# Softmax denominators from sums of three, three and two key blocks, added in wide pieces, in a two-pass attention kernel on one core

## What is computed

```
q = Wq @ layernorm(x) + bq;  k = Wk @ ctx + bk;  v = Wv @ ctx + bv     # 512 x 1024 each
dot  = mask * (q . k) / sqrt(32) - (1 - mask) * 1e6                    # per head, 1024 x 1024
out  = (softmax(dot) * mask) . v
x    = x + tanh(g_xattn) * out
y    = fp8(layernorm(x) * scale) / scale
x    = x + tanh(g_ffn) * (y @ (fp8(W2 * scale1) / scale1))
```

## Time and profile before

| | |
|---|---|
| median of 3 runs | 2537.36 us (2537.34 to 2537.48) |
| span of the profiled execution | 2538.4 us |
| PE busy | 2479.6 us, 98% of the span |
| DVE busy | 1986.1 us, 78% |
| POOL busy | 1642.1 us, 65% |
| ACT busy | 1392.0 us, 55% |
| DMA engines, mean share in the attention slices | 4 to 5 tenths |

### The profile page before, as it was taken

How to read it: one execution, slowest core, us unless ns; L and a number is a source line. 1 busy time by engine, 2 the same in 40 slices (tenths; PEclk the granted TensorE clock), 3 DMA queues, 4 the chain that set the end, 5 groups by cost and what they waited for, 6 DMA issues and landing times.

```text
span 2538.4 us, 40565 instructions
## 1 busy us (share of the span) xinstructions
PE 2479.6 (98%) x13177; PEld 1380.4 (54%) x13177; DVE 1986.1 (78%) x3259; ACT 1392.0 (55%) x2606; POOL 1642.1 (65%) x1259
## 2 busy tenths in 40 slices
PE   7999999999999999999999999999999999999997
PEld 5888888874444444444444444444444444444442
DVE  6767667776788888888888888888888888888885
ACT  3333333315666665666666666666665666666664
POOL 2333333426777777777777777777777777777775
PEclk9999999999999999999999999999999999999999
DMA  6766666653444444444444444444444444444411
GB/s 239 256 244 239 237 237 237 215 183 88 94 97 97 100 102 94 96 91 94 91 97 93 91 91 91 91 91 90 99 91 92 95 99 100 97 98 99 101 47 55
DMA packets 241807, 313.48 MB, mean 123 GB/s; under 512 B 75000, under 2 KB 142648, under 8 KB 241624
## 3 DMA queue, kind: packets, MB, share of 16 engines
q1 hardware_dynamic: 230776, 275.56, 43.2%
q10 hardware_dynamic: 10848, 35.66, 3.9%
HBM read 199.83 MB, written 101.38 MB: 119 GB/s over the span
## 4 chain that ended last, share of the span: by engine, by line
PE 88%; DVE 6%; issue 3%; DMA 1%; POOL 1%; ACT 0%; SPq 0%; DVEq 0%; POOLq 0%; ACTq 0%
PE bank L863 20%; PE bank L848 20%; PE bank L893 19%; PE bank L878 17%; PE bank L904 8%; PE bank L941 4%; DVE part_max L1146 3%; PE bank L933 1%; POOL pair_sum L398 1%; DMA q_st<-qx_scr 0%; DVE y L101 0%; DMA w_nat<-in_L_xattn_Wk_dram 0%; DMA v_scr<-stage 0%; DVE isnan L100 0%; DVE x_raw L1046 0%
## 5 line engine op out<-in xcount | busy, mean ns | idle before, releaser
L398 POOL TENSOR_TENSOR pair_sum<-probs 128x512 f32<-128x512 f32 x1020 | 1279.6, 1287 | 430.8 <-ACT probs L715 430.8
L1146 DVE TENSOR_REDUCE part_max<-bank 128x1 f32<-128x512 f32 x2048 | 1283.0, 682 | 346.4 <-PE bank L878 338.1
L715 ACT ACTIVATE probs<-bank 128x512 f32<-128x512 f32 x2048 | 1071.3, 603 | 655.8 <-PE bank L863 647.4
L863 PE MATMUL bank<-q_st,k_st 100*128 100x512 f32 x2048 | 875.4, 429 | 5.2 <-ACT probs L715 5.2
L878 PE MATMUL bank<-k_st,q_st 98*128 98x512 f32 x2048 | 814.0, 397 | 8.7 <-DVE part_max L1146 6.2
L863 PEld LDWEIGHTS bank<-q_st,k_st 100*128 100x128 f32 x2048 | 386.5, 189 | 513.2 <-issue 270.8
L893 PE MATMUL bank<-probs,v_t 128*32 128x512 f32 x4096 | 546.3, 605 | 0.0
L878 PEld LDWEIGHTS bank<-k_st,q_st 98*128 98x128 f32 x2048 | 388.7, 190 | 112.6 <-DVE part_max L1146 8.7
L389 POOL TENSOR_TENSOR stage_lo<-stage,stage_hi 128x512 fp32r<-128x512 f32 x128 | 185.4, 1473 | 139.5 <-ACT stage_hi L661 138.6
L904 PE MATMUL bank<-pair_sum,ones 128*32 128x512 f32 x2040 | 266.4, 594 | 0.0
L661 ACT ACTIVATE stage_hi<-stage 128x512 fp32r<-128x512 f32 x128 | 80.2, 632 | 205.7 <-DVE stage L1010 143.1
(11 more groups left out here) (112 smaller groups left out, 1969.1 us busy)
## 6 DMA issues: line engine op xcount, KB each, us to landing
k_st<-k_scr SPq DMA_DIRECT2D x96, 512.0 KB
q_st<-q_scr SPq DMA_DIRECT2D x192, 256.0 KB
c_raw<-in_ctx_dram ACTq DMA_DIRECT2D x32, 512.0 KB, 7.1
k_scr<-stage_hi SPq DMA_DIRECT2D x64, 256.0 KB, 2.5
k_scr<-stage_lo SPq DMA_DIRECT2D x64, 256.0 KB, 2.8
v_scr<-stage SPq DMA_DIRECT2D x64, 256.0 KB, 2.9
q_scr<-stage_hi SPq DMA_DIRECT2D x64, 256.0 KB, 2.3
q_scr<-stage_lo SPq DMA_DIRECT2D x64, 256.0 KB, 2.5
```

The costliest lines, as they stand in the source:

```text
L398: nc.gpsimd.tensor_tensor(pair_sum[:, r % 2, h], probs[:, a, h], probs[:, a + 1, h], ALU.add).then_inc(pair_done, 1)
L715: nc.scalar.activation(probs[:, c % PR, h, :], s_bank_of(n, k)[:, :], ACT.Exp).then_inc(exp_done, 1)
L863: nc.tensor.matmul(s_bank_of(n, k)[:, :], k_st[p][0:KS, h, j * P:(j + 1) * P], q_st[p][0:KS, th, h, :], start=True, stop=True).then_inc(sc ...
L1146: nc.vector.tensor_reduce(part_max[:, th, sh, at:at + 1], x_bank_of(n, "tile", k)[:, :], AX, ALU.max).then_inc(max_done, 2)
```

## The change

- `add_pair` becomes `add_block`. The eight key blocks of a half are summed as (0, 1, 2), (3, 4, 5), (6, 7). The second block of a group is added to the first, out of `probs`, the third to the running `group_sum`. Each block is added in two pieces of two heads, 128 x 1024. That is 5 blocks, 10 pieces in a half, 20 in a quad.
- Denominator bursts: three for a half, at slots 19, 35, 43, 59 and, in the next quad, 3 and 11: 6 in a quad instead of 8. ACT's wait for a free place in `probs` goes by the new count of adds (`ADDED`).
- In `slot`, PV and denominator bursts now come ahead of `turn_max` and `ffn`. A half of the feed-forward product is 8 matmuls in one piece behind the PV burst of slot 31 and of 47; DVE's `add_ffn` moves to the same slots.
- `weigh` is cut in two halves of 128 x 512, one behind POOL's block 2, one behind block 7 together with the residual.
- `stack_q` is split by halves: half 0 of quad n+2 is loaded in quad n, behind `load_v`; half 1 of quad n+1 at the quad's start as before. Semaphores are split to match.
- `NORM_AT`, `NORM_AT_2`, `negate_max` and `invert` on DVE stay where they are.

```diff
-            F_JOBS = {23: "max1", 34: "ffn0", 50: "ffn1", 55: "max0"}
+            GROUPS = ((0, 1, 2), (3, 4, 5), (6, 7))
+            F_JOBS = {23: "max1", 31: "ffn0", 47: "ffn1", 55: "max0"}
+            DEN_AT = {19: 0, 35: 1, 43: 2, 59: 3}
+            DEN_AFTER = {3: 4, 11: 5}
...
-                        for h in range(QH):
-                            pool.wait_ge(exp_done, NSLOT * n + 2 * QH * r + QH + h + 1)
-                            nc.gpsimd.tensor_tensor(pair_sum[:, r % 2, h], probs[:, a, h], probs[:, a + 1, h],
-                                                    ALU.add).then_inc(pair_done, 1)
+                        pool.wait_ge(exp_done, NSLOT * n + QH * c + 2 * half + 2)
+                        if opening is None:
+                            pool.wait_ge(sum_done, ADDS * (TH * n + th) + ADDED[j] - 4 + half + 1)
+                            before = group_sum[:, r % 2, hs]
+                        else:
+                            before = probs[:, (th * SJ + opening) % PR, hs]
+                        nc.gpsimd.tensor_tensor(group_sum[:, r % 2, hs], before, probs[:, c % PR, hs],
+                                                ALU.add).then_inc(sum_done, 1)
...
+                        if real(n) and real(n + 2):
+                            stack_q(n + 2, 0, p)
                         if real(n):
                             move_den(n, 0)
...
-                        for half, at_ in ((0, FFN_AT[0]), (1, FFN_AT[1])):
-                            if k in (at_, at_ + 1) and ordinary(n - 2):
-                                ffn(n, at_, n - 2, half, range(4 * (k - at_), 4 * (k - at_) + 4))
                         if k % 4 == 3:
...
+                        if k in DEN_AT and real(n):
+                            denominators(n, DEN_AT[k])
...
+                        if k in FFN_AT and ordinary(n - 2):
+                            ffn(n, k, n - 2, FFN_AT.index(k))
```

More of the change, by code:

```diff
@@ L176, in flamingo_gated_layer @@
         init_done = sem("init_done")
-        stacked = [sem(f"stacked{i}") for i in range(TH)]
+        k_stacked = sem("k_stacked")
+        q_stacked = [sem(f"q_stacked{i}") for i in range(TH)]
         v_loaded = [sem(f"v_loaded{i}") for i in range(2)]
@@ L194, in flamingo_gated_layer @@
         inv_moved = sem("inv_moved")
-        inv_spread = sem("inv_spread")
+        inv_spread = [sem(f"inv_spread{i}") for i in range(TH)]
         tm_loaded = sem("tm_loaded")
         res_loaded = [sem(f"res_loaded{i}") for i in range(2)]
+        half_weighed = sem("half_weighed")
         norm_done = sem("norm_done")
@@ L242, in flamingo_gated_layer @@
             PR = 4
+            GROUPS = ((0, 1, 2), (3, 4, 5), (6, 7))
+            NG = TH * len(GROUPS)
+            ADDS_AT = {}
+            for gi, blocks in enumerate(GROUPS):
+                for place in range(1, len(blocks)):
+                    ADDS_AT[blocks[place]] = (gi, blocks[0] if place == 1 else None)
+            ADDED = {}
+            ADDS = 0
+            for j_ in range(SJ):
+                if j_ in ADDS_AT:
+                    ADDS += 2
+                    ADDED[j_] = ADDS
+                else:
+                    ADDED[j_] = ADDS + 2
             XLEAD = 19
@@ L401, in weigh, with add_block @@
[L401 to L408, removed]
+                    def add_block(n, c, half):
+                        th, j = c // SJ, c % SJ
+                        gi, opening = ADDS_AT[j]
+                        r = th * len(GROUPS) + gi
+                        hs = slice(2 * half, 2 * half + 2)
+                        if opening is not None and half == 0 and counted(NG * n + r - 1):
+                            pool.wait_ge(den_done, NG * n + r - 1)
+                        pool.wait_ge(exp_done, NSLOT * n + QH * c + 2 * half + 2)
+                        if opening is None:
+                            pool.wait_ge(sum_done, ADDS * (TH * n + th) + ADDED[j] - 4 + half + 1)
+                            before = group_sum[:, r % 2, hs]
+                        else:
+                            before = probs[:, (th * SJ + opening) % PR, hs]
+                        nc.gpsimd.tensor_tensor(group_sum[:, r % 2, hs], before, probs[:, c % PR, hs],
+                                                ALU.add).then_inc(sum_done, 1)
@@ new lines, in weigh @@
+                    def weigh(m, th):
+                        pool.wait_ge(o_copied, 2 * m + th + 1)
+                        pool.wait_ge(inv_spread[th], 16 * (m + 1))
+                        if th == 0:
+                            if m > 0:
+                                pool.wait_ge(norm_done, NORM_STEPS * (m - 1) + 13)
+                            done = half_weighed
+                        else:
+                            if m > 0:
+                                pool.wait_ge(norm_done, NORM_STEPS * m)
+                            done = norm_done
+                        nc.gpsimd.tensor_tensor(y[:, th * HALF:(th + 1) * HALF], o_raw[:, th], inv_b[:, th],
+                                                ALU.mult).then_inc(done, 1)
```

146 lines of the change are left out of this document (77 added, 69 removed).

## The result

The changed kernel takes **3052.4 us** (median of 4 runs, 3043.7 to 3064.9), beside 2537.4 for the kernel before on the same chip: ratio 1.2032, 95% interval 1.2001 to 1.2063. It is slower by 515 us. The forecast was 2955, in a range of 2760 to 3080. The profiled execution has a span of 3050.3 us.

A forecast was written before the change was run, and what follows sets the result against it. PE was taken to bound the kernel, with 88% of the chain that ended last. 2537 - 55 (denominators) - 10 (turn and product) + 375 (stops) + 109 (clock) = 2956, say 2955 us; range 2760 to 3080.

The forecast's parts named there:

- two denominator bursts a quad less: On PE, two denominator bursts a quad, 64 in all, go at 0.86 us each: -55 us.
- turn and feed-forward product: Behind a PV burst, up to 0.25 us saved for each of 64 turns, nothing to speak of for the product: -10 us.
- early load: Query stacks of half 0 loaded one quad sooner, ahead of move_den: moved at no cost, 0 us.
- stops of PE: PE stands still for DVE ahead of slots 23 and 55, 12.1 us in each of 31 quads: +375 us.
- half clock: PE at 1.2 GHz after its stops, 1.5 losses of 2.35 us a quad: +109 us, between 0 and 190.
- Slot 51: Three DVE instructions wait 4.6 us for POOL's adds, so PE stops 4.3 us ahead of slot 55.
- Rival 1: DVE's 16-column L1160 does not wait for a running add: about 2790 us, chance 0.22.
- Slot 19: Five DVE instructions in a row wait for POOL's wide adds; PE stands still about 7.8 us ahead of slot 23.
- 3.5 passes: At slot 19, four DVE instructions behind the first let adds of POOL pass, 2.07 us each: 7.3 us.
- rival 2: PE's clock holds through the pauses, with no half clock: about 2845 us, chance 0.14.
- third rival: The forecast's name in its clock term for PE's clock holding, the sum then 109 us lower; listed as rival 2.
- Rival 3: DVE is not held back by POOL's adds and only the gain stands: 2472 us, faster, chance 0.08.

The follow-up runs named there:

- e_behind_before: The kernel before, with only the turn of the maxima and the feed-forward product (with add_ffn) moved behind the PV bursts; 2500.8 us, ratio 0.9853.
- e_narrow: The changed kernel with the same sums added head by head in 128 x 512 pieces instead of 128 x 1024; 2931.7 us.
- e_busy23: The changed kernel with 36 matmuls without a use on PE in slot 23, where it would stand still; 2984.6 us.
- e_gates_inv: The changed kernel with POOL's adds held back as in e_gates, and DVE's invert moved from slots 23 and 55 to 19 and 51; 2545.1 us, ratio 1.0031.
- e_gates: The changed kernel with POOL's adds held back at slots 19 and 51 until DVE has negated its maxima; 2638.3 us, ratio 1.0417.
- e_weigh7: The changed kernel with both halves of weigh behind block 7, none ahead of the four adds at slot 19; 3022.9 us.

## Why the prediction was right, and where it was not

**Direction, place and size.** PE's stops stand where they were put, ahead of slots 23 and 55, put down to the reduction behind DVE's negation, and the gates prove their cause. The terms, measured (turn and early load in other kernels than the changed one):

| term | forecast | measured |
|---|---|---|
| two denominator bursts a quad less | -55 | -53 (2.41 to 1.55 and 2.53 to 1.68, x 31) |
| turn and feed-forward product | -10 | -36.5 (e_behind_before) |
| early load | 0 | -6 |
| stops of PE | +375 | +402 |
| half clock | +109 | about +204 |
| sum | +419 | +510 |

The measured terms make 510 of the 515 us. The clock's is the one that no run measured as a whole; it comes from the distances between slots, below. That the total missed by 97 us only is in part luck: the clock's term was 95 too low and the stops' 27, while a gain from turn and product that was 26 larger than forecast, and the 6 of the early load, took part of it back.

**Denominators.** Right, to 2 us.

**Turn and product, mis-sized.** "Nothing to speak of for the product" was read from the 0.24 us of its eight matmuls. The distance that counts is the whole slot's: a half of the product in two pieces between tiles cost 0.20 to 0.24 us more than in one piece behind a burst, and a turn 0.37, where at most 0.25 stood.

**Slot 51.** Right as a mechanism: L1209, L1214 and L1216 wait for one add each, and the stop is 4.18 where 4.3 stood. Rival 1 falls with L1214: a 16-column instruction waits 2.29 us.

**Slot 19, near by its sum and wrong by its step.** "3.5 passes" of 2.07 us over five instructions, 7.8 us for PE, was taken from the alternation in the earlier trace rows. In 26 of 30 quads one instruction is passed by four adds instead and four instructions wait for nothing, with a stop of mostly 8.8 to 9.3 us. In the 4 quads that alternate as I described, the stop is 8.05 to 8.23. Either way DVE is held for about four adds, so the sum was near though the step was wrong. What decides between the two ways I didn't have, and it is still open. The width of an add, which carried the sum, is borne out at both slots by e_narrow.

The Trainium skill (SBUF — State Buffer, Who interferes with whom) says that whoever issues first gets the shared pair (the SBUF ports that VectorE and GpSimd share) for the whole instruction. L1214 at 2.29 us and the reductions at 0.68 beside an add, unhindered, agree with its list of what contends. By issue order, L1209 of 1188.04 would go ahead of the add of 1188.46; the trace shows that one and three more going first. Here the measurement decides.

**The clock, mis-sized.** "One loss a quad for the longer stop and half a one for the shorter", at 2.35 us each, made 3.5 us. Against an undisturbed quad (e_behind_before without the two bursts), slots 23 to 31 are longer by 12.16 us, of which 8.86 are the stop, and slots 55 to 60 by 7.45, of which 4.18 are: 3.3 us behind each, 6.57 in a quad, 204 in all. The shorter stop costs a whole loss too, and my upper bound of 190 was passed. For slot 23 e_busy23 bears this out (2.62 of the 3.30 us in a quad); for slot 55 it rests on distances alone.

**Two slips in the working.** A clock that holds is rival 2 of the list, not the "third rival". And the upper end of the range adds 65 us for "all losses of clock", where the term's own bounds give 190 - 109 = 81, which makes 3096 instead of 3080; the result lies under both.

**Rival 3** is what the gates approach: without the waits the quad would be 59.67 - 0.86 - 0.85 = 58.0. e_gates_inv stands at 61.08, so in none of these kernels did the wide sums earn what their two saved bursts are worth, while turn and product alone gave 36.5 us.

## What to carry to other kernels

Before you give POOL longer or more closely packed work, list DVE's instructions that read two inputs from SBUF, and its `tensor_scalar` ones (L1214, L100 and, in e_gates_inv, L90 waited here), the small ones first, and see what stands behind each: here waits that fell mostly on 16-column instructions held up PE for 402 us. Look whether POOL's work comes in one unbroken piece over them, for then one DVE instruction can wait for all of it; a rest in the chain, here 0.14 to 0.17 us by a wait on its own last result, let DVE in. And test the parts of a change alone: one part was worth 1.5% and the whole cost 20%.

## What the runs showed that I had not expected

- A waiting DVE instruction was passed by four POOL adds in a row: 9.73 us with wide adds, 6.07 with narrow ones (at another slot), 8.22 without `weigh` ahead of them. At slot 51 of the same kernel, and at slots 23 and 55 of e_gates, it was passed by the running add only. Breaking the chain at slot 19 by 0.14 to 0.17 us ended the long wait. Why a chain just as tight at slot 51 lets DVE in is open. It is not that POOL is further behind ACT at slot 19: in e_weigh7 it is about as close there as at slot 51, and passes DVE all the same. Nor is it the place alone, since at slot 19 of the changed kernel DVE got in after each add in 4 of 30 quads, and with narrow adds in all 24.
- An instruction of 0.17 us (L1214, 16 columns, one SBUF input) waits for a whole add like a large one.
- Pauses of 4.2 us, once a quad in otherwise full work, cost PE as much clock as pauses of 9 us: about 3.3 us each. In e_gates pauses of 1.5 us ahead of slot 27 too were followed by a granted clock of 0.50, while those of 0.8 and 1.1 us in e_gates_inv were not.
